# Per-tile sums in two column halves, bias by ScalarE, turn by transposition, and 7 instead of 6 of 32 tiles on TensorE, in a graph-attention kernel on Trainium2

## What is computed

```
Q, K, V = x @ Wq.T + bq, x @ Wk.T + bk, x @ Wv.T + bv      # (N, 64)
Ee      = edge_attr @ We.T + be                            # (E, 64)
score   = exp(clip((K[src] * Q[dst] * 0.25 * Ee).sum over each head's 16, -5, 5))
msg     = V[src] * score
out     = layernorm(x + segment_sum(msg, dst))
```

## Time and profile before

| | us |
|---|---|
| median of 3 runs | 1717.57 (1716.67 to 1718.51) |
| the profiled execution | 1715.64 |
| its span, first to last instruction | 1713.8 |
| TensorE busy (products) | 1649.7, 96% |
| VectorE busy | 1318.6, 77% |
| ScalarE busy | 960.6, 56% |
| GpSimd busy | 1263.1, 74% |

### The profile page before, as it was taken

The page is one execution under the profiler, slowest core; times in us unless marked ns, Lnnn a source line. Parts: engine busy times, 40 slices in busy tenths (PEclk is TensorE's granted clock), DMA queues, the critical chain, the costliest instruction groups (busy, mean ns, idle before and its releaser), DMA issues. The chain is left out here.

```text
span 1713.8 us, 47297 instructions
## 1 busy us (share of the span) xinstructions
PE 1649.7 (96%) x13047; PEld 1479.4 (86%) x13047; DVE 1318.6 (77%) x2198; ACT 960.6 (56%) x2864; POOL 1263.1 (74%) x1348
## 2 busy tenths in 40 slices
PE   7399999999999999999999999999999999999994
PEld 7298888888888888888888988888888888888884
DVE  6377878778778778778778778778778787787786
ACT  5355555555555556556556556556555555555554
POOL 4677777777777777777777777777777777777774
PEclk8699999999999999999999999999999999999997
DMA  7455554555554555555555555455445555545441
GB/s 240 126 149 132 144 134 131 145 133 132 144 133 133 143 132 135 140 135 135 138 135 137 133 138 139 133 137 138 134 131 145 134 131 144 133 132 145 132 124 62
DMA packets 198830, 234.44 MB, mean 137 GB/s; under 512 B 96742, under 2 KB 123180, under 8 KB 198684
## 3 DMA queue, kind: packets, MB, share of 16 engines
q1 hardware_dynamic: 156732, 147.96, 30.0%
q0 software_dynamic: 42080, 86.26, 20.9%
HBM read 226.67 MB, written 7.38 MB: 137 GB/s over the span
## 5 line engine op out<-in xcount | busy, mean ns | idle before, releaser
L260 POOL DMA_INDIRECT kv<-kv_table,idx x1315 | 1246.1, 948 | 416.5 <-issue 388.1
L654 PE MATMUL xg_bank<-x_hi,src_onehot 128*128 128x448 f32 x2079 | 786.4, 378 | 6.1 <-DVE src_onehot L786 6.1
L655 PE MATMUL xg_bank<-x_lo,src_onehot 128*128 128x448 f32 x2079 | 759.9, 365 | 0.0
L725 ACT ACTIVATE distance<-iota_w,dst_neg 128x64 f32<-128x64 f32 x1612 | 428.4, 339 | 0.0
L654 PEld LDWEIGHTS xg_bank<-x_hi,src_onehot 128*128 128x128 f32 x2079 | 391.8, 188 | 34.6 <-DVE src_onehot L786 6.3
L655 PEld LDWEIGHTS xg_bank<-x_lo,src_onehot 128*128 128x128 f32 x2079 | 392.3, 189 | 27.3
L751 ACT COPY xg_t_sb<-turn_bank 64x256 f32<-64x256 f32 x198 | 61.9, 313 | 616.9 <-PE turn_bank L665 612.1
L798 DVE SCALAR_TENSOR_TENSOR x_sel<-iota_v,src_block,xg_bank 128x448 f32<-128x448 f32 x297 | 202.0, 680 | 248.5 <-PE xg_bank L655 240.7
L786 DVE TENSOR_TENSOR src_onehot<-r_row,xg_bank 128x896 fp32r<-128x896 f32 x297 | 320.0, 1078 | 24.8 <-DMA r_row<-r_table 24.8
L643 PE MATMUL sum_ps<-onehot,msg 128*64 128x64 f32 x3224 | 224.4, 223 | 8.6 <-DVE msg L843 8.6
L643 PEld LDWEIGHTS sum_ps<-onehot,msg 128*64 128x64 f32 x3224 | 208.9, 138 | 17.2 <-DVE msg L843 9.4
(11 more groups left out here) (116 smaller groups left out, 957.8 us busy)
## 6 DMA issues: line engine op xcount, KB each, us to landing
attr_sb<-attr SPq DMA_DIRECT2D x201, 256.0 KB
dst_row<-dst_rows SPq DMA_DIRECT2D x402, 128.0 KB
kv<-kv_table,idx POOLq DMA_INDIRECT x1315
r_row<-r_table SPq DMA_DIRECT2D x99, 128.0 KB
q_win<-q_table SPq DMA_DIRECT2D x404, 24.0 KB
r_row<-r_table SPq DMA_DIRECT2D x99, 64.0 KB
idx<-src_tab SPq DMA_DIRECT2D x206, 4.0 KB, 4.1
kv_table<-kv_stage SPq DMA_DIRECT2D x7, 448.0 KB, 3.8
```

The lines of the kernel that those rows point to most:

```text
L260: pool.indirect_dma_start(out=kv[:, slot, t, :], out_offset=None, in_=kv_table, in_offset=bass.IndirectOffsetOnAxis(ap=idx[:, slot, t:t + ...
L654: pe.matmul(xg, src_onehot[:, parity, u, :], x_hi[:, u, :], start=(u == 0), stop=False)
L655: mm = pe.matmul(xg, src_onehot[:, parity, u, :], x_lo[:, u, :], start=False, stop=(u == U - 1))
L725: made = act.activation(distance[:, t, :], iota_w[:, :], ACT.Square, bias=dst_neg[:, ds(g, 1), t:t + 1].rearrange("p o t -> p (o t)"))
```

## The change

Four things, and what they need around them:

1. `sum_messages` writes the even tiles' sums to partitions 0 to 63 and the odd tiles' to 64 to 127 of the same bank (the upper half of the array's columns), and VectorE adds both halves to `acc`: the second addition stands after kqe.
2. The bias in float32 is copied into the PSUM bank by ScalarE (`seed_edges`, right after the exponential, for two groups ahead); the attributes' products add onto it, and the 512-column product is gone. TensorE waits for that copy instead of for kqe. Two 512-column products before the second stage open the two banks. GpSimd's preparation of the bias in three parts is gone.
3. `turn_x` is a transposition; its operand is padded with zeros from 64 to 128 columns.
4. Tiles on TensorE by slot: 2, 2, 2, 1 instead of 2, 1, 2, 1. The loops of TensorE and VectorE are unrolled over two turns, since 7 is odd and two buffers alternate by tile.

```diff
-PE_BEFORE = (0, 2, 3, 5)
-PE_EACH = 6
+PE_OF = (2, 2, 2, 1)
+PE_BEFORE = (0, 2, 4, 6)
+PE_EACH = sum(PE_OF)
...
-            return 0 if isinstance(g, int) and not PE_FROM <= g < PE_END else 2 - slot % 2
+            return 0 if isinstance(g, int) and not PE_FROM <= g < PE_END else PE_OF[slot]
...
+                for i in range(2):
+                    pe.matmul(bank(ee_ps[i], 512), ones[:, :], q_win[...][:, 0:512],
+                              start=True, stop=True).then_inc(ee_opened, 1)
...
-                        if not (isinstance(g, int) and g < 2):
-                            pe.wait_ge(kqe_made, g - 1)
+                        pe.wait_ge(ee_seeded, g + 1)
                         ee = bank(ee_ps[slot % 2], n * P)
-                        pe.matmul(ee, ones[:, :], be_sb[:, 0:2 * n, :].rearrange("p t f -> p (t f)"),
-                                  start=True, stop=False)
                         for k in range(n):
                             mm = pe.matmul(ee[:, k * P:(k + 1) * P], attr_sb[:, slot, k * P:(k + 1) * P],
-                                           we_sb[:, :], start=False, stop=(k == n - 1))
+                                           we_sb[:, :], start=False, stop=True, skip_group_check=True)
...
                         for t in range(n):
-                            mm = pe.matmul(sum_ps[0:F, slot % 2, 0:W], msg[:, slot % 2, t, :],
-                                           onehot[:, slot, t, :], start=(t == 0), stop=(t == n - 1))
+                            half = slice(t % 2 * F, (t % 2 + 1) * F)
+                            mm = pe.matmul(sum_ps[half, slot % 2, 0:W], msg[:, slot % 2, t, :],
+                                           onehot[:, slot, t, :], start=(t < 2), stop=(t >= n - 2))
...
                         for n in range(k):
-                            mm = pe.matmul(turn_bank[0:F, n, :], xg_sb[:, j % 2, n, :], ident[:, :], start=True, stop=True)
+                            mm = pe.transpose(turn_bank[:, n, :], xg_sb[:, j % 2, n, :], ident[:, :])
...
+                    def seed_edges(g, slot):
+
+                        if not (isinstance(g, int) and g < 2):
+                            act.wait_ge(kqe_made, g - 1)
+                        act.copy(ee_ps[slot % 2][:, :, :], be_f[:, :].unsqueeze(1).to_broadcast([P, T, F]))\
+                           .then_inc(ee_seeded, 1)
...
                         act.activation(p_ps[:, 0:n], score_c[:, 0:n], ACT.Exp).then_inc(exp_made, 1)
+                        if ahead:
+                            seed_edges(g + 2, slot2)
...
                         if not (isinstance(g, int) and g == 0):
-                            dve.wait_ge(acc_added, g)
+                            dve.wait_ge(acc_added, 2 * g)
...
+                    def add_odd_sums(g, slot, nodes):
+
+                        dve.wait_ge(acc_added, 2 * g + 1)
+                        dve.tensor_tensor(acc[:, nodes], acc[:, nodes], sum_ps[F:2 * F, slot % 2, 0:W],
+                                          ALU.add).then_inc(acc_added, 1)
...
                         dve.tensor_tensor(kqe[:, 0:n, :], kq[:, 0:n, :], ee_ps[slot % 2][:, 0:n, :],
                                           ALU.mult).then_inc(kqe_made, 1)
+                        if not (isinstance(g, int) and g == 0):
+                            add_odd_sums(g - 1, (slot - 1) % SLOTS, nodes)
...
-                    with dve.Fori(1, ITERS - 1) as i:
-                        for j in range(SLOTS):
-                            step(i * SLOTS + j, i, j)
+                    with dve.Fori(0, (ITERS - 2) // 2) as two:
+                        for h in range(2):
+                            for j in range(SLOTS):
+                                step(two * (2 * SLOTS) + ((h + 1) * SLOTS + j), two * 2 + (h + 1), j, (h + 1) % 2)
```

More of the change, by code:

```diff
@@ L72, in gnn_kernel @@
         q_table = nc.dram_tensor("q_table", [NPAD, 3 * F], BF16, kind="Internal").ap()
-        r_table = nc.dram_tensor("r_table", [1, Q * P], F32, kind="Internal").ap()
+        r_table = nc.dram_tensor("r_table", [1, QROWS * 3 * P], F32, kind="Internal").ap()
         w_sb = sb("w_sb", [P, 3 * F], F32)
@@ L249, in first_q, with parity_of @@
             return (i + j // SLOTS) * PE_EACH + PE_BEFORE[j % SLOTS] - PE_SKIPPED
+        def parity_of(odd, j, k):
+            return ((odd + j // SLOTS) * PE_EACH + PE_BEFORE[j % SLOTS] - PE_SKIPPED + k) % 2
         def gathered(slot, turn):
@@ L254, in gathered @@
                 return sum(pool_tiles(t * SLOTS + slot, slot) for t in range(turn + 1))
-            return turn * (T - 2 + slot % 2) + pool_tiles(slot, slot)
+            return turn * (T - PE_OF[slot]) + pool_tiles(slot, slot)
         def gather(pool, g, slot, first=0, end=T):
@@ L325, in _ @@
                 pool.wait_ge(iota_set, 5)
[L327 to L340, removed]
                 pool.wait_ge(idx_first, 16 * SLOTS)
@@ L379, in _ @@
                     mm.then_inc(q_computed, 1)
+                pe.wait_ge(kv_staged[0], CHUNKS)
+                pe.wait_ge(kv_staged[1], CHUNKS)
+                pe.wait_ge(consts_zeroed, 3)
+                for i in range(2):
+                    pe.matmul(bank(ee_ps[i], 512), ones[:, :], q_win[:, :, :, :, :].rearrange("p a b c d -> p (a b c d)")[:, 0:512],
+                              start=True, stop=True).then_inc(ee_opened, 1)
+                pe.wait_ge(ee_opened, 2)
             @block.scalar
@@ L673, in project, with step @@
                         mm.then_inc(kv_projected, 1)
-                    def step(g, i, j):
+                    def step(g, i, j, odd):
                         last = isinstance(g, int) and g + 1 == G
@@ L682, in step @@
                         for k in range(ahead)[0:1]:
-                            gather_x(first_q(i, j + 2), (PE_BEFORE[(j + 2) % SLOTS] - PE_SKIPPED) % 2)
+                            gather_x(first_q(i, j + 2), parity_of(odd, j + 2, 0))
                         turned = pe_tiles(g + 1, (j + 1) % SLOTS)
@@ L690, in step @@
                         for k in range(ahead)[1:2]:
-                            gather_x(first_q(i, j + 2) + 1, (PE_BEFORE[(j + 2) % SLOTS] - PE_SKIPPED + 1) % 2)
+                            gather_x(first_q(i, j + 2) + 1, parity_of(odd, j + 2, 1))
+                    pe.wait_ge(xg_padded, 1)
                     multiply_edges(0, 0, 0)
@@ L695, in _ @@
                     for g in range(SLOTS):
-                        step(g, 0, g)
-                    with nc.Fori(1, ITERS - 1, engines=[pe.engine], hint_back_edge=True) as i:
-                        for j in range(SLOTS):
-                            step(i * SLOTS + j, i, j)
+                        step(g, 0, g, 0)
+                    with nc.Fori(0, (ITERS - 2) // 2, engines=[pe.engine], hint_back_edge=True) as two:
+                        for h in range(2):
+                            for j in range(SLOTS):
+                                step(two * (2 * SLOTS) + ((h + 1) * SLOTS + j), two * 2 + (h + 1), j, (h + 1) % 2)
                     for g in range((ITERS - 1) * SLOTS, G):
-                        step(g, g // SLOTS, g % SLOTS)
+                        step(g, g // SLOTS, g % SLOTS, g // SLOTS % 2)
                 @block.scalar
@@ L777, in _, with make_src_onehot @@
                 def _(dve):
-                    def make_src_onehot(g, i, j, k):
+                    def make_src_onehot(g, i, j, k, odd):
                         q, slot = first_q(i, j) + k, j % SLOTS
-                        parity = (PE_BEFORE[slot] - PE_SKIPPED + k) % 2
+                        parity = parity_of(odd, j, k)
                         if k == 0:
@@ L848, in step @@
                         if pe_tiles(g + 2, (j + 2) % SLOTS):
-                            select_x(g + 2, i, j + 2, 0)
+                            select_x(g + 2, i, j + 2, 0, odd)
                         if pe_tiles(g + 3, (j + 3) % SLOTS):
-                            make_src_onehot(g + 3, i, j + 3, 0)
-                    make_src_onehot(PE_FROM, 0, PE_FROM, 0)
+                            make_src_onehot(g + 3, i, j + 3, 0, odd)
+                    dve.memset(xg_sb[:, :, :, F:2 * F], 0.0).then_inc(xg_padded, 1)
+                    make_src_onehot(PE_FROM, 0, PE_FROM, 0, 0)
                     for g in range(SLOTS):
-                        step(g, 0, g)
-                    with dve.Fori(1, ITERS - 1) as i:
-                        for j in range(SLOTS):
-                            step(i * SLOTS + j, i, j)
+                        step(g, 0, g, 0)
+                    with dve.Fori(0, (ITERS - 2) // 2) as two:
+                        for h in range(2):
+                            for j in range(SLOTS):
+                                step(two * (2 * SLOTS) + ((h + 1) * SLOTS + j), two * 2 + (h + 1), j, (h + 1) % 2)
                     for g in range((ITERS - 1) * SLOTS, G - 1):
-                        step(g, g // SLOTS, g % SLOTS)
+                        step(g, g // SLOTS, g % SLOTS, g // SLOTS % 2)
```

(5 more changed lines are left out.)

46 lines of the change are left out of this document (24 added, 22 removed).

## The result

The changed kernel takes 1720.84 us (median of 19 runs, 1719.18 to 1723.12), the kernel before 1716.67 (19 runs, 1715.10 to 1718.51): a ratio of 1.0025, 95% interval 1.0018 to 1.0031. It is slower by 4.2 us; 12.4 were forecast. The profiled execution took 1721.81 us, 1719.6 from first to last instruction.

The account below looks back on a forecast made before the run. TensorE and GpSimd were taken as both full, VectorE close behind. TensorE's 33.68 us a turn, less 1.68 for sums, plus 0.56 wait, gives 32.56: +0.27, times 49 +13 us, so 1730 us; 8-in-10 range 1697 to 1796.

Parts of the forecast that it names:

- GpSimd as second full engine: GpSimd's 26 gathers a turn take 32.46 us, so a cheaper TensorE alone gains almost nothing; 25 gathers need 31.2 us.
- Bias: On TensorE, dropping the bias product saves 0.22 us four times a turn: -0.88.
- Seventh tile, +3.09: On TensorE, one more tile a turn costs +2.87 us for its gather and +0.22 for its projection.
- Sums and turn, -1.68 and -0.82: On TensorE, sums in two halves save 0.42 us a group, -1.68 a turn; turning by transposition saves 0.82 a turn.
- the end of the range: Saving from overlapping sums on TensorE, between 0 and 0.47 us a group; 0.42 was taken, near the upper end.
- my upper bound: A transposition on TensorE costs between 0.06 and 0.11 us; 0.08 was taken.
- The wait, 0.56: Once a turn, before the group with one TensorE tile, TensorE's sum waits 0.56 us for VectorE's message.
- its bound: The wait for the message lies between 0.1 us (no overlap of the sums) and 0.8 us.
- loads serialize: Rival: the sums' halves on TensorE gain nothing, +1.53 us a turn, 1792 us; chance 0.18, wholly or for the larger part.
- Ends: First stage about +0.5 us on VectorE and tail -1, together -0.5 us.

Follow-up runs that it names:

- experiment 8: The changed kernel with six tiles a turn on TensorE (2, 1, 2, 1 by slot) instead of seven: 1717.32 us, ratio 0.9993 to the kernel before.
- experiment 2: The changed kernel with all sums in partitions 0 to 63 again and without VectorE's second addition: 1805.62 us.
- experiments 1 and 10: The changed kernel with VectorE's second one-hot moved behind the message in the critical step: 1700.40 us; the same with sums in one half: 1785.10 us.
- experiments 1 and 11: The changed kernel with VectorE's second one-hot behind the message: 1700.40 us; with that one-hot cut in two, 2 blocks before the message, 5 behind: 1693.54 us.
- experiment 4: The changed kernel with the turn by a product with the identity again instead of the transposition: 1762.91 us.
- experiment 9: The changed kernel with sums of tiles 0 to 3 in the lower half and 4 to 7 in the upper, not alternating: 1777.46 us.
- experiments 1 to 4 and 9 to 12: Those listed here except experiment 8, plus the changed kernel with the bias product on TensorE again (1756.53 us) and a repeat of the later one-hot (1701.29 us).

## Why the prediction was right in kind and off in size

The direction, the causes and the range held; the forecast of +12.4 us was three times the measured +4.2. All stretches of TensorE between groups 3 and 199, added up from both traces, in us a turn:

| from start to start | before | after | change | forecast |
|---|---|---|---|---|
| edges, with the bias, to Q | 4.45 | 3.56 | -0.89 | -0.88 |
| Q to the gather | 2.57 | 2.57 | 0 | 0 |
| gathers, first to last product | 16.37 | 18.99 | +2.62 | |
| last product of a second gather to the edges | 0.41 | 0.60 | +0.19 | |
| projection to what follows | 1.59 | 1.73 | +0.14 | |
| these three, the seventh tile | | | +2.95 | +3.09 |
| last gather product to the sums, without the wait | 2.74 | 1.96 | -0.79 | -0.82 |
| sums to the projection | 4.16 | 2.46 | -1.70 | -1.68 |
| wait for the message | 0 | 0.58 | +0.58 | +0.56 |
| all | 32.29 | 32.45 | +0.16 | +0.27 |

- **GpSimd as second full engine**: right (experiment 8).
- **Bias**: right; putting it back costs 0.71 a turn plus the 0.21 by which the wait shrinks.
- **Seventh tile, +3.09: too large by 0.14, and this is the step that failed.** I took the length of a gather from the trace of before for all seven. At that length the tile costs 3.08 (2.73 for its products, 0.21 behind them, 0.14 at the projections). But every gather of the changed kernel takes 2.713 us from first to last product on average, where it took 2.728: seven times -0.015 is -0.11, and the rest is 0.02 behind the last products. I had no reason to expect it, and what causes it stays open (below).
- **Sums and turn, -1.68 and -0.82: right, but in part by luck.** Two errors inside them all but cancel. The products of the sums save 0.46 a group (1.075 in experiment 2, 0.615 with halves) and not 0.42, 0.16 more a turn: it is the full half. I had stayed short of the end of the range for caution, with no row for it. The Trainium skill ("TensorEngine Tiling (Array Packing)", Key Properties: tiles load and multiply in parallel) gives this end; the rule of "TensorE: Matmul & The Clock Gate", Part 3, that loads overlap running products only across row groups, would give none of it, and these runs are against it. A transposition in turn costs 0.108 from start to start (my upper bound) and not 0.08, 0.20 more a turn. I had scaled the transpositions of the last stage from half clock to the full one; but those move 64 columns and these 128, which the rows show and I passed over. In the table neither error is seen, since 0.14 of the turn's own cost (the 0.05 behind the first narrow product, which I had left with the turn) now lies in the sums.
- **The wait, 0.56: right**: 0.58, once a turn, in the step named, for the reason named (experiments 1 and 10). But its bound was argued wrongly: I held it at 0.1 without overlap, and experiment 2 shows 0.43, since VectorE's chain lengthens with the sums. The rival "loads serialize" was therefore priced too low, at 1792; experiment 2, which has the sums in one half, takes 1805.
- **Ends**: -0.5 forecast, -1.9 measured.

So a forecast of +0.27 a turn, the difference of 3.65 us added and 3.38 removed, was nearly halved by 0.14 in one term. The 0.11 by which the turn is shorter than forecast is 5.5 us; with 1.4 at the ends that is 6.9 of the 7.2 between the profiled spans' difference (+5.8) and the forecast (+13). The runs' median difference, +4.2, lies 1.6 lower still, within the scatter of single runs (3 to 4 us from lowest to highest).

The change gains nothing for a plain reason: TensorE's own work falls from 32.29 to 31.87 a turn, though it does a tile more, and the message comes 0.58 later than it could be used. With that wait gone (experiments 1 and 11) the same change gains 1%, and 1.4%.

## What to carry to other kernels

Where two engines are full and a third has no slack in one step of the loop, ask at each part of a change what is taken from the stretch that ends in that step; it is paid back there. The step with the least work on the bottleneck engine between two waits is where the next chain appears; reorder what the dependent engine does ahead of the awaited instruction before saving more. And when a forecast is a small difference of large terms, give each term its own error before giving a size: here 0.5% on the length of a gather, seven times a turn, was most of the miss.

## What the runs showed of the hardware

- Products of 64 stationary columns whose outputs lie in different halves of the partitions run as two streams: in the records pairs start 6 to 7 ns apart, and the next pair 58 ns later, where one half alone takes 58.5 ns a product. From the first to the last of the 16 it is 0.464 us, against 0.924 in one half (experiment 2): the full factor of two, reached by alternating tiles, with the two instructions of a float32 product left side by side in the code.
- Products of different halves are not kept in program order (experiment 4: a sum product starts 0.10 us ahead of the last turn product in every free step, 148 times), and the look-ahead is short (experiment 9, about three products).
- TensorE's stall of about 0.1 us on the way from 128 to 64 stationary columns is there in both kernels: 0.30 instead of 0.20 ahead of the first turn product before, 0.20 instead of 0.108 ahead of the first sum product after.
- The gather's products are 0.201 us apart in the median from the first kind to the second in all kernels with seven tiles, and 0.204 in the kernel before and in experiment 8, with six. Experiment 8 has the unrolled loops and the three other parts too, so it is not these. The tables' size and all addresses behind them differ with the number of tiles. This was not separated.
- In experiment 8, where TensorE waits 2.3 us a turn, its granted clock fell to half 14 times between 440 and 1590 us, each time for a few microseconds (0.98 in the mean of that stretch); in the traces of experiments 1 to 4 and 9 to 12 and in both kernels it is 1.00 from 100 to 1650 us.
